# A hybrid transformer block on one core: variance plus epsilon, negated mean and shift of every layer normalisation are computed on GpSimd instead of VectorE

## What is computed

```python
x = x + attention(layernorm(x))            # causal, one head, Q = K-fold, V
x = x + moe(layernorm(x))                  # 32 experts of width 64, top 4, plus a shared expert of 128
x = x + rwkv(layernorm(x))                 # time mix: ln1 of it, decay scan, then channel mix with ln2
x = x + moe(layernorm(x))
def layernorm(x): return (x - mean) / sqrt(var + 1e-5)
```

## Time and profile before

| | |
|---|---|
| time, median of 3 runs | 825.12 us (823.36 to 825.74) |
| profiled execution: span of its instructions | 824.9 us; no other time is given for it |
| TensorE busy | 808.0 us, 98% |
| VectorE busy | 658.5 us, 80% |
| ScalarE busy | 548.2 us, 66% |
| GpSimd busy | 600.9 us, 73% |

### The profile page before, as it was taken

One profiled execution on the slowest core, in us unless ns is written; L12 is line 12 of the kernel. 1 busy time (PEld: TensorE's weight loads), 2 busy tenths in 40 slices (PEclk: granted clock), 3 DMA queues, 4 the chain that ended last, 5 costly groups with the idle time before them and its releaser, 6 DMA issues. The chain is left out here.

```text
span 824.9 us, 12552 instructions
## 1 busy us (share of the span) xinstructions
PE 808.0 (98%) x3782; PEld 604.1 (73%) x3782; DVE 658.5 (80%) x1533; ACT 548.2 (66%) x1016; POOL 600.9 (73%) x469
## 2 busy tenths in 40 slices
PE   7899999999999999999999999999999999999997
PEld 4577878667677676677778777777777767888785
DVE  4887777898897998988777877978778889765664
ACT  3567677776657767679474884749666675777453
POOL 2158878767858677588777886877878787968775
PEclk9999999999999999999999999999999999999999
DMA  9062624425244063351554507255262534426553
GB/s 321 22 132 56 145 60 106 103 47 123 52 106 101 18 139 80 88 118 29 111 111 106 128 7 153 62 117 130 53 134 60 126 82 106 99 52 123 120 115 76
DMA packets 49331, 80.73 MB, mean 98 GB/s; under 512 B 3280, under 2 KB 14544, under 8 KB 48880
## 3 DMA queue, kind: packets, MB, share of 16 engines
q1 hardware_dynamic: 48976, 79.72, 42.1%
q10 hardware_dynamic: 288, 0.20, 0.1%
HBM read 75.19 MB, written 4.72 MB: 97 GB/s over the span
## 5 line engine op out<-in xcount | busy, mean ns | idle before, releaser
L490 POOL TENSOR_TENSOR m_h<-m_v,m_wb 128x512 f32<-128x512 f32 x256 | 347.8, 1369 | 128.5 <-DVE m_v L1222 50.9
L580 ACT ACTIVATE m_th<-pa 128x512 f32<-128x512 f32 x240 | 142.0, 595 | 144.9 <-PE pa L848 133.2
L1222 DVE TENSOR_TENSOR m_v<-m_th,pb 128x512 f32<-128x512 f32 x224 | 151.2, 677 | 35.3 <-ACT m_th L580 15.3
L844 PE MATMUL pa<-m_xh,w1h 128*128 128x512 f32 x272 | 149.2, 548 | 0.0
L337 POOL TENSOR_TENSOR m_hl<-m_h,m_hh 128x512 fp32r<-128x512 f32 x84 | 109.8, 1307 | 37.0 <-ACT m_hh L745 36.8
L745 ACT ACTIVATE m_hh<-m_h 128x512 fp32r<-128x512 f32 x171 | 107.0, 626 | 22.3 <-POOL m_h L490 21.4
L844 PE MATMUL pb<-m_xh,w3h 128*128 128x512 f32 x272 | 113.8, 418 | 1.0 <-DVE m_v L1222 0.8
L845 PE MATMUL pa<-m_xh,w1l 128*128 128x512 f32 x272 | 107.9, 397 | 0.0
L845 PE MATMUL pb<-m_xh,w3l 128*128 128x512 f32 x272 | 107.7, 396 | 0.0
L848 PE MATMUL pb<-m_xl,w3h 128*128 128x512 f32 x272 | 107.5, 395 | 0.0
L848 PE MATMUL pa<-m_xl,w1h 128*128 128x512 f32 x272 | 107.5, 395 | 0.0
(11 more groups left out here) (273 smaller groups left out, 1625.3 us busy)
## 6 DMA issues: line engine op xcount, KB each, us to landing
m_wb<-w_scratch SPq DMA_DIRECT2D x126, 512.0 KB, 6.8
x_sb<-in_x SPq DMA_DIRECT2D x8, 256.0 KB, 7.1
m_wb<-in_w SPq DMA_DIRECT2D x2, 1024.0 KB, 7.1
x_out<-x_sb SPq DMA_DIRECT2D x7, 256.0 KB, 6.8
u_scratch<-t_u SPq DMA_DIRECT2D x6, 256.0 KB, 2.5
t_u<-u_scratch SPq DMA_DIRECT2D x6, 256.0 KB, 2.8
f_kk<-in_w SPq DMA_DIRECT2D x1, 1024.0 KB, 10.0
w_scratch<-r_wT SPq DMA_DIRECT2D x16, 64.0 KB, 1.5
```

Source lines behind the costliest of these rows:

```text
L490: pool.tensor_tensor(hidden(g, p), gated(g, p), m_wb[:, p % (GRING * GP), :], ALU.mult).then_inc(sig["m_h"], 1)
L580: ins = act.activation(m_th[:, p % 2, :], pa[p % 2][:, :], ACT.Silu)
L844: pe.matmul(ps[:, :], high[:, p, :], xh, start=True, stop=False)
L1222: dve.tensor_tensor(gated(g, p), m_th[:, r, :], pb[r][:, :], ALU.mult).then_inc(sig["m_v"], 1)
```

## The change

The helper `scales` takes the place of `rsqrt` on GpSimd. It waits for the statistics, adds epsilon, negates the mean, waits for its own two results, makes the power, waits for it, and multiplies it into the negated mean. VectorE keeps the statistics, which now wait until the shift that was read from the same buffers one round earlier is done, and loses `shifts` and the additions of epsilon. For the time mix GpSimd makes two sums of 128x4, two negated means, one power of 128x8 and one product of 128x8. GpSimd's slots stay where they were. The statistics stay at their slots on VectorE.

```diff
--- before.py
+++ after.py
@@ -472,9 +472,15 @@
             pool.affine_select(out=spread[:, :, :], in_=spread[:, :, :], compare_op=ALU.is_ge, fill=0.0, base=H - 1,
                                pattern=[[-P, GP], [-1, P]], channel_multiplier=H).then_inc(sig["c_pool"], 1)
 
-            def rsqrt(out, in_, ready, n, signal):
-                pool.wait_ge(sig[ready], n)
-                pool.tensor_tensor(out, in_, minus_half[:, 0:out.shape[1]], ALU.pow).then_inc(sig[signal], 1)
+            def scales(rs, nm, ve, mv, s_mvs, s_ve, s_rstd, s_nm, n):
+
+                pool.wait_ge(sig[s_mvs], n)
+                pool.tensor_scalar(ve, mv[:, :, 1], EPS, None, ALU.add).then_inc(sig[s_ve], 1)
+                pool.tensor_scalar(nm, mv[:, :, 0], -1.0, None, ALU.mult).then_inc(sig[s_ve], 1)
+                pool.wait_ge(sig[s_ve], 2 * n)
+                pool.tensor_tensor(rs, ve, minus_half[:, 0:T], ALU.pow).then_inc(sig[s_rstd], 1)
+                pool.wait_ge(sig[s_rstd], n)
+                pool.tensor_tensor(nm, nm, rs, ALU.mult).then_inc(sig[s_nm], 1)
 
             def unit(g, p):
 
@@ -492,11 +498,11 @@
 
             def att_step(n, slot, mode):
                 if slot == (5, 15, 8, 8)[mode]:
-                    rsqrt(a_rs[:, :], a_ve[:, :], "a_vedone", n + 1, "a_rstd")
+                    scales(a_rs[:, :], a_sh[:, :], a_ve[:, :], a_mv, "a_mvs", "a_vedone", "a_rstd", "a_sh", n + 1)
 
             def pro_step(q, slot, mode):
                 if slot == (13, 6, 3, 11, 6, 11, 2, 31)[mode]:
-                    rsqrt(r_rs[:, :], r_ve[:, :], "r_vedone", q + 1, "r_rstd")
+                    scales(r_rs[:, :], r_nm[:, :], r_ve[:, :], r_mv, "r_mvs", "r_vedone", "r_rstd", "r_nm", q + 1)
                 if slot == (29, 19, 28, 28, 38, 42, 32, 31)[mode]:
                     pool.wait_ge(sig["r_xT"], q + 1)
                     pool.wait_ge(sig["m_xh"], q + 1)
@@ -505,7 +511,16 @@
 
             def time_begin(m, slot, mode):
                 if slot == (0, 0, 2)[mode]:
-                    rsqrt(t_rs[:, :], t_ve[:, :], "t_ve", 2 * m + 2, "t_rstd")
+                    pool.wait_ge(sig["t_mvs"], m + 1)
+                    pool.tensor_scalar(t_ve[:, 0:T], t_mv[:, :, 1], EPS, None, ALU.add).then_inc(sig["t_ve"], 1)
+                    pool.tensor_scalar(t_ve[:, T:2 * T], t_mv[:, :, 1], 1.0 + EPS, EPS * EPS, ALU.mult, ALU.add)\
+                        .then_inc(sig["t_ve"], 1)
+                    pool.tensor_scalar(t_nm[:, 0:T], t_mv[:, :, 0], -1.0, None, ALU.mult).then_inc(sig["t_ve"], 1)
+                    pool.tensor_scalar(t_nm[:, T:2 * T], t_mv[:, :, 0], -1.0, None, ALU.mult).then_inc(sig["t_ve"], 1)
+                    pool.wait_ge(sig["t_ve"], 4 * m + 4)
+                    pool.tensor_tensor(t_rs[:, :], t_ve[:, :], minus_half[:, :], ALU.pow).then_inc(sig["t_rstd"], 1)
+                    pool.wait_ge(sig["t_rstd"], m + 1)
+                    pool.tensor_tensor(t_nm[:, :], t_nm[:, :], t_rs[:, :], ALU.mult).then_inc(sig["t_nm"], 1)
                 if slot == (19, 13, 19)[mode]:
 
                     pool.wait_ge(sig["t_h"], m + 1)
@@ -527,7 +542,7 @@
                     pool.tensor_tensor(wide(chunk(m)), wide(chunk(m)), wide(t_u2[:, :, :]), ALU.add)\
                         .then_inc(sig["f_x"], 1)
                 if slot == (7, 15, 20, 16)[mode]:
-                    rsqrt(a_rs[:, :], a_ve[:, :], "f_ve", m + 1, "f_rstd")
+                    scales(a_rs[:, :], f_nm[:, :], a_ve[:, :], a_mv, "f_mvs", "f_ve", "f_rstd", "f_nm", m + 1)
                 if slot == (20, 21, 30, 29)[mode]:
                     pool.wait_ge(sig["f_h"], m + 1)
                     pool.tensor_tensor(f_d[:, :], f_h[:, 1:1 + S], f_h[:, 0:S], ALU.subtract).then_inc(sig["f_d"], 1)
@@ -585,7 +600,7 @@
             def att_step(n, slot, mode):
                 if slot == (14, 22, 0, 7)[mode]:
                     if n > 0:
-                        act.wait_ge(sig["a_sh"], n)
+                        act.wait_ge(sig["a_sh"], n + 1)
                         act.wait_ge(sig["a_tr"], n)
                         normalise(a_xn, chunk(n), a_rs, a_sh, "a_xn")
                 if slot == (16, 35, 0, 7)[mode]:
@@ -658,7 +673,7 @@
             def time_begin(m, slot, q, mode):
                 if slot == (12, 9, 13)[mode]:
                     vectors_loaded()
-                    act.wait_ge(sig["t_nm"], 2 * m + 2)
+                    act.wait_ge(sig["t_nm"], m + 1)
                     normalise(t_hn, chunk(m), t_rs[:, T:2 * T], t_nm[:, T:2 * T], "t_hn")
                 if slot == (19, 13, 20)[mode]:
                     vectors_loaded()
@@ -1182,11 +1197,6 @@
                 ins.then_inc(sig[s_mv], 1)
                 dve.wait_ge(sig[s_mv], n + 1)
 
-            def shifts(dst, mv, rs, signal):
-
-                dve.scalar_tensor_tensor(out=dst, in0=mv[:, :, 0], scalar=-1.0, in1=rs, op0=ALU.mult,
-                                         op1=ALU.mult).then_inc(sig[signal], 1)
-
             def normalise(dst, src, mv, rs, signal):
 
                 for t in range(T):
@@ -1237,14 +1247,11 @@
                 if slot == (0, 17, 0, 1)[mode]:
                     if n < 2:
                         dve.wait_ge(sig["in_x1" if n else "in_x0"], 16)
+                    wait(dve, "a_sh", n)
                     row_stats(chunk(n), a_st, a_mv, n, "a_stats", "a_mvs")
-                    dve.tensor_scalar(a_ve[:, 0:T], a_mv[:, :, 1], EPS, None, ALU.add).then_inc(sig["a_vedone"], 1)
-                if slot == (11, 19, 0, 6)[mode]:
-                    dve.wait_ge(sig["a_rstd"], n + 1)
                     if n == 0:
+                        dve.wait_ge(sig["a_rstd"], n + 1)
                         normalise(a_xn, chunk(n), a_mv, a_rs, "a_xn")
-                    else:
-                        shifts(a_sh[:, :], a_mv, a_rs[:, :], "a_sh")
                 if slot == (28, 35, 1, 25)[mode]:
                     row_max(n, 0, (0, 1), (0, P))
                 if slot == (37, 40, 3, 29)[mode]:
@@ -1328,11 +1335,8 @@
                         dve.wait_ge(sig["a_add"], 3 * q + 3)
                     else:
                         dve.wait_ge(sig["f_x"], 2 * (q - B) + 2)
+                    wait(dve, "r_nm", q)
                     row_stats(chunk(sequence(q)), r_st, r_mv, q, "r_stats", "r_mvs")
-                    dve.tensor_scalar(r_ve[:, :], r_mv[:, :, 1], EPS, None, ALU.add).then_inc(sig["r_vedone"], 1)
-                if slot == (20, 14, 14, 19, 15, 13, 10, 19)[mode]:
-                    dve.wait_ge(sig["r_rstd"], q + 1)
-                    shifts(r_nm[:, :], r_mv, r_rs[:, :], "r_nm")
                 if slot == (30, 24, 29, 28, 22, 32, 17, 26)[mode]:
 
                     dve.wait_ge(sig["r_lgps"], q + 1)
@@ -1391,14 +1395,8 @@
 
 
                     dve.wait_ge(sig["m_x"], m + 1)
+                    wait(dve, "t_nm", m)
                     row_stats(chunk(m), t_st, t_mv, m, "t_stats", "t_mvs")
-                    dve.tensor_scalar(t_ve[:, 0:T], t_mv[:, :, 1], EPS, None, ALU.add).then_inc(sig["t_ve"], 1)
-                    dve.tensor_scalar(t_ve[:, T:2 * T], t_mv[:, :, 1], 1.0 + EPS, EPS * EPS, ALU.mult,
-                                      ALU.add).then_inc(sig["t_ve"], 1)
-                if slot == (8, 5, 11)[mode]:
-                    dve.wait_ge(sig["t_rstd"], m + 1)
-                    shifts(t_nm[:, T:2 * T], t_mv, t_rs[:, T:2 * T], "t_nm")
-                    shifts(t_nm[:, 0:T], t_mv, t_rs[:, 0:T], "t_nm")
                 if slot == (22, 24, 23)[mode]:
 
                     if m in MIXED:
@@ -1487,11 +1485,8 @@
                     dve.memset(f_h[:, 0:1], 0.0).then_inc(sig["f_zero"], 1)
                 if slot == (9, 16, 21, 17)[mode]:
                     kept(dve, m)
+                    wait(dve, "f_nm", m)
                     row_stats(t_u2, a_st, a_mv, m, "f_stats", "f_mvs")
-                    dve.tensor_scalar(a_ve[:, 0:T], a_mv[:, :, 1], EPS, None, ALU.add).then_inc(sig["f_ve"], 1)
-                if slot == (13, 21, 28, 23)[mode]:
-                    dve.wait_ge(sig["f_rstd"], m + 1)
-                    shifts(f_nm[:, :], a_mv, a_rs[:, 0:T], "f_nm")
                 if slot == (23, 27, 35, 32)[mode]:
                     dve.wait_ge(sig["f_d"], m + 1)
                     for dst, c in ((f_xk, FMIX_K), (f_xr, FMIX_R)):

```

## The result

The changed kernel takes 881.5 us (median of 4 runs, 880.2 to 881.9) where the kernel before takes 824.3 (4 runs beside them, 823.4 to 825.7): 1.068 times as long, with an interval of 1.067 to 1.070. That is 57 us slower, against a forecast of 825.4 and a range up to 829. The profiled execution spans 880.1 us, so 55.2 us lie between the two profiles.

A forecast was written before the change was run, and what follows sets the result against it. TensorE was taken to bound the kernel from 45 to 820 us, a chain of small steps the opening. 824.9 + 0.25 (opening) + 0 (passes) = 825.15, plus 0.2 for the median: 825.4 us, 8-in-10 range 822.8 to 829.

The forecast's parts named there:

- The bound: From 45 to 820 us TensorE is busy 769.83 of 775.00 us; other engines' steps count only if TensorE waits.
- Term 3: The passes from 45 us on: 0, bounds -2.6 to +3 us; pass 6 worst, GpSimd's lateness and ScalarE's earlier start cancel.
- The bound of idle time: From 45 to 820 us, some 5.2 us of TensorE idle time are all a faster partner can give back.
- The held work: VectorE's sums and shifts, 31.0 us, mostly no work: held while GpSimd runs, 922 ns for attention's shift against 150.
- Small instructions: GpSimd's new 128x4 additions and products were priced at 150 ns each, bounds 109 and 295 ns.
- The forecast of 26: GpSimd's load over the kernel grows by 136 x 0.15 + 80 x 0.07 = 26 us, bounds 20 and 46.
- Term 1: Opening, attention of sequence 0: GpSimd's power starts at 6.71 us, 0.1 us later; bounds 0 and +0.4.
- Term 2: Opening, router of sequence 0: +0.15 us (0 to +0.6), from +0.12 before the power and +0.03 behind it.
- VectorE no longer waits 1.12 us there: Opening, router: nothing comes of VectorE's lost wait, since the row maximum behind its weight splits waits for TensorE anyway.
- The slower one: Dear small instructions, 0.5 us each, make TensorE wait about 1.3 us in passes 6, 8, 10, 12: 830.9 us, chance 0.14.
- the second rival: VectorE's relief reaches TensorE in the passes: 822.6 us or a little under, faster, chance 0.10.
- First use: Opening: GpSimd's first addition may fetch its code, 825.6 us, or 831 with about 6 us; over 2.5 us, chance 0.03.

The follow-up runs named there:

- e14_dummies_6on: The kernel before, GpSimd given scratch instructions and self-waits of the change's number, kinds and sizes, from pass 6 on alone: 841.8 us.
- e16_dose12: The kernel before with twelve small scratch instructions on GpSimd right in front of `t_n` in passes 2 to 5: 852.0 us.
- e4_opening_wait: The changed kernel with VectorE waiting at slot 19 of the opening for the router's shift of sequence 0, as before the change: 876.6 us.
- e7_xl_att_late: The changed kernel; in passes 2 to 5 GpSimd's `m_xl` moves from slot 19 to 28 and attention's scales from 15 to 20: 893.3 us.
- e8_filler: The changed kernel with 18 filler matmuls on TensorE ahead of its wait for `r_lg` in passes 2 to 5: 871.9 us.
- e10_att_late_opening: The changed kernel; passes 2 to 5: attention's scales at slot 24, ScalarE's normalisation at 30; opening: VectorE waits for the router's shift: 872.6 us.
- e15_dose3: The kernel before with three small scratch instructions on GpSimd right in front of `t_n` in passes 2 to 5: 828.2 us.

## Why the prediction was wrong

**The bound.** Right: a step on another engine counts only where it makes TensorE wait. The error is in what came next, "a slower partner costs nothing until its lateness has eaten the lead that it has over the down projection". That is the lead of one of GpSimd's outputs. `t_n` is another output, and it has no lead: VectorE already waited for it 0.35 us before the change, and TensorE's product started 0.15 us behind `r_lg`.

**Term 3, the step that failed.** "Pass 6 is the worst for GpSimd" took the pass with the most normalisations and asked when `m_hl` is due. Passes 2 to 5 have three as well, and lost 30.9 us where the term had 0 (at most 3 for all). The bound of idle time (5.2 us of the earlier trace rows) says what can be won, and I let it stand for what can be lost. Pass 6 itself lost 3.4 us, also by mixes: `t_xk` 1.76, `t_xv` 1.59, `a_p` 1.16 and `a_pT` 1.77 us, where one was held before, and behind them `f_xl`, for which TensorE waits 7.7 us in four passes (6, 8, 10 and 12). The chain there was read off the time line and is shown by e14_dummies_6on only as far as its cause is GpSimd's time.

**The held work.** The prediction quoted the hold to explain why VectorE's shifts were cheap to remove. The Trainium skill (SBUF — State Buffer, "Who interferes with whom") adds, of VectorE's two-port modes, that the instruction that issues first keeps the shared access and the other blocks fully. The mixes, which have two inputs, behave the same here: `t_xk` starts 0.08 us behind `m_xl` and takes 1.75 us instead of 0.75. Who comes next after the first is not always the one that waited: in pass 3 the two engines take turns, while in e16_dose12 one mix waited through three instructions of GpSimd. What I missed is that hold time doesn't vanish with the instruction that showed it. VectorE lost 31 us of groups and only 9 in all, because the hold moved on to the mixes: seven each of `t_xk`, `t_xv` and `t_xr` took 33.2 us instead of 18.4, and the channel mix's `a_p` and `a_pT` 6.2 us more.

**Small instructions.** 0.15 us was too low. Alone they take 0.23 us (negation, bounded it at 0.109 and 0.295) and 0.20 (product), 0.31 from one start to the next beside a wait; a whole set takes 1.95 us where the power alone took 1.01. The reading that led to the low price, that the power's length goes with its columns and hardly anything is fixed, doesn't hold either: in pass 3 after the change four columns take 1.04 us and eight 1.67. The sums of the router take 429 ns on average, held. GpSimd's busy time rose by 33 us. The forecast of 26 counted 5.6 us of waiting, which is not busy time, so 20.4 us of work were forecast; with its bounds up to 46 us the term was inside its range.

**The opening.** Term 1 forecast the power at 6.7 us, with 7.0 as upper bound; it starts at 7.03. Term 2 was +0.15 us. GpSimd's own part is 0.55 (e4_opening_wait), within the bounds. The rest, 2.9 us between ScalarE's starts, came from the sentence "VectorE no longer waits 1.12 us there", after which I looked at what VectorE waits for next and not at whom it holds meanwhile. Another 1.7 us between ScalarE's start and pass 0 are the clock, for which the prediction had no term. With the wait the time fell by 5.0 us.

**The rivals.** The slower one had the right sign, the wrong place and a tenth of the size (6 of 57 us): it had lateness arrive one for one. (The prediction calls the hold of GpSimd the second rival's mechanism; it belongs to this one.) Its wait for `m_hl` did come, but in pass 14, once, and there it was followed by a lower clock too:

```profile
PE py L890 <- POOL m_hl L337: 2.1, 1, 2.1
```

Pass 14 takes 42.3 us instead of 38.4, at a granted clock of 0.96 instead of 1.00. In all five kernels that take 40.6 us or more for it (the change itself, e4_opening_wait, e7_xl_att_late, e8_filler and e10_att_late_opening) TensorE waits 1.5 to 2.1 us for `m_hl` there; in the thirteen others, with 38.4 to 39.1 us, it doesn't. This was read from the profiles and not tested by a change of that wait. First use cost nothing: the first sum took 0.25 us. The 6 us that the Trainium skill (GPSIMD Engine Reference, 2.1 "Instruction dispatch") gives for the first call of a freshly loaded kernel are not seen here.

**Still open.** Why `m_hl` is late in pass 14 in some kernels and not in others, what each wait in passes 6 to 13 is worth, and why the opening ahead of the router's statistics differs by 2 us were not taken apart. No kernel tried here beats the one before.

## What to carry to other kernels

Before work is put on an engine with idle time, list every output of that engine that someone waits for, and find the smallest slack among them, pass by pass; a mean load of 73% says nothing, and `t_n` had none. Where two engines share an access, look also at which of their instructions now start to overlap: a gap of 1.8 us on GpSimd was what made three mixes of VectorE cheap. When a wait is removed, ask what the engine will do in that time and whom it holds. And try a dose first: three scratch instructions in front of the suspect would have shown the slope.

## What the runs showed of the hardware

- A mix of 128x512 on VectorE takes 0.75 us alone and 1.75 beside a 1.3 us instruction of GpSimd; held over three of them it took 4.19.
- The hold goes both ways and doesn't need two inputs: GpSimd's negation of 128x4 took 2.14 us beside VectorE's split and a one-input cast of 128x2048, 0.23 without them.
- After a wait of 5 us TensorE ran at 1.2 GHz for part of the next 6 us (granted clock 0.60 there), worth 2.9 us a pass (e8_filler); waits of 1.4 to 1.6 us left the mean of passes 2 to 5 at 0.99 (e15_dose3).
- A GpSimd instruction of 128x4 takes 0.19 us in a row of twelve, and the power of four columns 1.04 (of eight 1.67): at this size the operation decides.
